# Holding back the second half of batch 1's stacks in the first attention's prologue

## The chip, the cores and the metric

The kernel runs on one core of one Trainium2 chip. The metric is the device time of one execution in microseconds (us). A core has TensorE (PE, matrix products and transposes into PSUM), VectorE (DVE), ScalarE (ACT), GpSimd (POOL) and SyncE (SP), each with an instruction stream of its own, joined by semaphores, and 16 DMA engines that all of them share. SP and POOL issue DMAs here.

## The reference

Two blocks of gated attention and feed-forward over x (8 batches of 256 tokens, width 256) and a context of the same shape. The change touches the first attention alone:

```
x = x + tanh(g_xattn[0]) * attention(layernorm(x), ctx, ctx)
  q = layernorm(x) @ Wq + bq;  k = ctx @ Wk + bk;  v = ctx @ Wv + bv       16 heads of 16
  softmax(q k^T / 4) v, heads side by side, @ Wo + bo
x = x + tanh(g_ffn[0]) * slots(layernorm(x))          (a routed slot layer with a GRU)
x = x + tanh(g_xattn[1]) * attention(layernorm(ctx), layernorm(ctx) and layernorm(x))
x = x + tanh(g_ffn[1]) * quantised gated feed-forward(layernorm(x))
```

All is float32. Products that need more precision than one pass gives are made from a high and a low part of each operand.

## The kernel before, in words

`attention0` runs over the 8 batches in order. For each batch the context and the normalised x are turned by PE and projected to k and q. ACT takes the high part out of PSUM (`k_high`, `q_high`, L393), DVE the low part (`k_low`, `q_low`, L553), which raises the semaphores `k_lo` and `q_lo`. Then DMAs from SBUF to SBUF build "stacks": for each pair of heads the 16 rows of q and k stand three times under each other (high with high, high with low, low with high), so that one matmul with 48 rows makes the precise product. `place` issues them: 64 KB each, two per row group, so six for k and six for q for one half of the head pairs (pairs 0 to 3 are half 0, pairs 4 to 7 half 1). A batch needs four such groups of six, 24 DMAs.

A batch has eight head pairs (r = 0 to 7). PE makes `scores` of a pair (L815), DVE takes the row maxima (`pair_max`, L568), POOL splits the maxima of two pairs into a high and a low part (`split_max`, L322 and L324), PE turns them (`turn_max`, L835), ACT copies them out (`shift_out`, L413) and POOL writes them by two small DMAs as two more rows of the query stack (`shift_in`, L330). The `shifted_scores` (L828) are then the transposed scores less the maximum, made from 50 rows; ACT takes their exponential (L407), and `group` (L846) multiplies by v. Scores run six pairs ahead of the transposed ones (`AHEAD = 6`), so at r = 2 of batch b the scores of pair 0 of batch b + 1 are made, at r = 6 those of its pair 4. `fold_bias` (L856, once, at r = 7 of batch 0) needs Wo and bo.

Every engine follows an order written out by hand. PE's prologue ends with `scores(0, 0, 0)` to `scores(0, 0, 5)` with two `turn_max` between them, and then the loop over batches begins with `shifted_scores(0, 0, 0)`. SP issues, in this order: ctx 0, x 0, weights, ctx 1, x 1, `first_stacks()` (half 0 of batch 0's k, the high rows of its q, half 1 of its q), ctx 2, x 2, `stacks(1, 1, False)` (both halves of batch 1), bo, Wo, w1, w2, ctx 3, x 3, `stacks(2, 0, True)`, and so on. POOL places the last row group of q for half 0 of batch 0 (two DMAs, `first_q`) and half 1 of its k (six, `first_k`). Between batches SP waits for `k_lo` and `q_lo` of the batch to be placed.

In the rows, the tiles of the two key stacks are `c_kv` (even batches) and `a_k_stack` (odd batches), the query stack is `a_q_stack`, the parts that they are copied from, and the shifts, lie in `w_hi` and `w_lo`, and PSUM is `ab_ps`.

Of the kernel before, what the change touches and what calls it, by code (L numbers as in the profile page):

```python
# [42 lines left out]
HP = 2  # L43
# [28 lines left out]
def wait(eng, sem, count):  # L72

    if isinstance(count, int) and count <= 0:
        return
    eng.wait_ge(sem, count)


def pause(eng, sem, count, passed):

    eng.wait_ge(sem, count)
    if not isinstance(count, int):
        eng.sem_inc(passed, 1)


def flat(ap):
    return ap.rearrange("p a d -> p (a d)")
# [13 lines left out]
def attention0(nc, a, x_sb, ident, gates, gru, slot, xn1, shared, xT_first, ps):  # L101
# [7 lines left out]
    with ctx:  # L109
# [21 lines left out]
        k_parts, q_parts = (part(0, 2048 * i, 2048).rearrange("p (a b n) -> p a b n", a=2, b=2) for i in range(2))  # L131
        k_stack = (shared[2][:, :, :, :].rearrange("p a c n -> p (a c n)").rearrange("p (r t) -> p r t", r=NR), sb("a_k_stack", [P, NR, T], F32R)[:, :, :])
        q_stack = sb("a_q_stack", [P, 2, NR, T], F32R)
# [26 lines left out]
        s = {k: sem("a_" + k) for k in names}  # L160
# [16 lines left out]
        def in_order(batch):  # L177

            for b in range(B):
                batch(b, b % 2, done=b > 0, prep=b < B - 2, more=b < B - 1, old=b > 1)  # L180

        K_ROWS = ((0, 0), (2, 0), (1, 1))
        Q_ROWS = ((0, 0), (1, 0), (2, 1))

        def rows_of(stack, par, rows):
            return stack[par][rows, :, :] if isinstance(stack, tuple) else stack[rows, par, :, :]

        def place(eng, parts, stack, which, half, par, done):

            for i, part in which:  # L190
                for e in range(HP):
                    eng.dma_start(rows_of(stack, par, slice(64 * e + DK * i, 64 * e + DK * i + DK))[:, 4 * half:4 * half + 4, :].bitcast(F32),
                                  parts[64 * e:64 * e + 64, par, part, half * T:(half + 1) * T].bitcast(F32)).then_inc(done, DMA)
# [9 lines left out]
        def _(sp):  # L203
# [8 lines left out]
            def stacks(n, par, again):  # L212
                for half in range(2):
                    if later(n):
                        pause(sp, s[("stack0", "stack1")[half]], HALF * n - (2 * DMA, HALF // 2)[half], s["sp_passed"])
                    if again:
                        pause(sp, s["ST"], HP * (NR * n - 3 * NR // 2 + half * NR // 2), s["sp_passed"])
                    if half == 0:
                        pause(sp, s["k_lo"], n + 1, s["sp_passed"])
                    place(sp, k_parts, k_stack, K_ROWS, half, par, s[("stack0", "stack1")[half]])  # L220
                    if half == 0:
                        pause(sp, s["q_lo"], n + 1, s["sp_passed"])
                    place(sp, q_parts, q_stack, Q_ROWS, half, par, s[("stack0", "stack1")[half]])
# [5 lines left out]
            def first_stacks():  # L229

                sp.wait_ge(s["k_hi"], 1)
                place(sp, k_parts, k_stack, K_ROWS[:2], 0, 0, s["stack0"])
                sp.wait_ge(s["k_lo"], 1)
                place(sp, k_parts, k_stack, K_ROWS[2:], 0, 0, s["stack0"])
                sp.wait_ge(s["q_hi"], 1)
                place(sp, q_parts, q_stack, Q_ROWS[:2], 0, 0, s["stack0"])
                sp.wait_ge(s["q_lo"], 1)
                place(sp, q_parts, q_stack, Q_ROWS, 1, 0, s["stack1"])

            load_ctx(0)  # L240
# [53 lines left out]
        @block.gpsimd  # L294
        def _(pool):
            nc.gpsimd.memset(ident[:, :], 0.0).then_inc(s["ident0"], 1)
            pool.wait_ge(s["ident0"], 1)
            nc.gpsimd.affine_select(out=ident[:, :], in_=ident[:, :], compare_op=ALU.not_equal, fill=1.0, base=0,
                                    pattern=[[-1, P]], channel_multiplier=1).then_inc(s["ident"], 1)
            pool.memset(minus_half4[:, :], -0.5).then_inc(s["const"], 1)  # L300
            pool.memset(unit[:, :], 1.0).then_inc(s["unit"], 1)
            pool.wait_ge(s["unit"], 1)
            for e in range(HP):
                for par in range(2):
                    pool.dma_start(k_stack[par][64 * e + 3 * DK:64 * e + 3 * DK + 2, :, :].bitcast(F32),
                                   unit[:, None, :].broadcast_to([2, NR, T])).then_inc(s["units"], DMA)
            pool.memset(max_parts[:, :, :, :].bitcast(F32), 0.0).then_inc(s["zeros"], 1)
            pool.memset(v_ones[:, :, :, :, DK:VW], 1.0).then_inc(s["ones"], 1)
            pool.wait_ge(s["const"], 1)

            def rstd_of(n):
                pool.wait_ge(s["var"], n + 1)
                wait(pool, s["xn"], n)
                nc.gpsimd.tensor_tensor(rstd[:, :], var_eps[:, :], minus_half[:, :], ALU.pow).then_inc(s["rstd"], 1)

            def split_max(G, buf):

                columns = max_parts[:, buf, :, :].rearrange("p t (e c) -> p t e c", e=HP)
                pause(pool, s["max"], 4 * G + 4, s["pool_passed"])
                if not isinstance(G, int) or G >= 2:  # L320
                    pause(pool, s["turned"], G - 1, s["pool_passed"])
                nc.gpsimd.tensor_copy(columns[:, :, :, 0:2], neg_max[:, buf, :, :, :]).then_inc(s["parts"], 1)  # L322
                pool.wait_ge(s["parts"], 2 * G + 1)
                nc.gpsimd.tensor_tensor(columns[:, :, :, 2:4], neg_max[:, buf, :, :, :], columns[:, :, :, 0:2].bitcast(F32), ALU.subtract).then_inc(s["parts"], 1)  # L324

            def shift_in(G, g, par):

                pause(pool, s["shift"], G + 1, s["pool_passed"])
                for e in range(HP):
                    pool.dma_start(q_stack[64 * e + 3 * DK:64 * e + 3 * DK + 2, par, 2 * g:2 * g + 2, :].bitcast(F32),  # L330
                                   shift[64 * e:64 * e + 4, g % 2, :].bitcast(F32)).then_inc(s[("shifted0", "shifted1")[g % 2]], DMA)

            rstd_of(0)
            rstd_of(1)
            pool.wait_ge(s["zeros"], 1)
            pool.wait_ge(s["q_lo"], 1)
            place(pool, q_parts, q_stack, Q_ROWS[2:], 0, 0, s["first_q"])
            pool.wait_ge(s["k_lo"], 1)
            place(pool, k_parts, k_stack, K_ROWS, 1, 0, s["first_k"])
            split_max(0, 0)  # L340
            shift_in(0, 0, 0)
            split_max(1, 1)
            shift_in(1, 1, 0)
            split_max(2, 0)

            def batch(b, par, done, prep, more, old):
                if prep:
                    rstd_of(b + 2)
                shift_in(4 * b + 2, 2, par)
                for g in range(3, 7 if more else 4):  # L350
                    split_max(4 * b + g, g % 2)
                    if g < 6:
                        shift_in(4 * b + g, g % 4, par if g < 4 else 1 - par)

            in_order(batch)
            for p in range(NPAIR - 1):
                t4 = slice(4 * p, 4 * p + 4)
                pool.wait_ge(s["slot_var"], p + 1)
                nc.gpsimd.tensor_tensor(slot["rstd"][:, t4], slot["var_eps"][:, t4], minus_half4[:, :], ALU.pow).then_inc(s["slot_rstd"], 1)
            pool.wait_ge(s["slot_rstd"], NPAIR - 1)  # L360
# [145 lines left out]
        def _(dve):  # L506
# [38 lines left out]
            def xnT_lo(n, bank):  # L545
                dve.wait_ge(s["xT_hi"], n + 1)
                nc.vector.tensor_tensor(xT_lo[:, :], bank[:, :], xT_hi[:, :].bitcast(F32), ALU.subtract).then_inc(s["xT_lo"], 1)
# [9 lines left out]
            def k_low(n, par, bank=pK):  # L557
                low(n, "k_hi", k_parts[:, par, :, :], bank, bkq[:, 0, :], "k_lo")

            def q_low(n, par, bank=pK):  # L560
                low(n, "q_hi", q_parts[:, par, :, :], bank, bkq[:, 1, :], "q_lo")

            def pair_max(n, G, r):

                wait(dve, s["parts"], 2 * G - 2)
                for e in range(HP):
                    dve.wait_ge(s["S"], 2 * n + e + 1)
                    nc.vector.tensor_reduce(neg_max[:, r // 2 % 2, :, e, r % 2], pS[:, e, :, :], AX_X, ALU.max, negate=True).then_inc(s["max"], 1)  # L568
# [161 lines left out]
            nc.vector.tensor_copy(bv_wide[:, :, :], bv_col[:, :, None].broadcast_to([P, DC, P])).then_inc(s["bvw"], 1)  # L730
            xnT_lo(1, flat(pT[:, 1, :, :]))
            k_low(1, 1, pP)
            q_low(1, 1, pK)
            pair_max(0, 0, 0)
            pair_max(1, 0, 1)
            pair_max(2, 1, 2)
            pair_max(3, 1, 3)
# [2137 lines left out]
```

## Time and profile before

| | us |
|---|---|
| median of 3 runs (lowest, highest) | 858.06 (855.92, 859.29) |
| the profiled execution, its own time | 858.11 |
| its span, first to last instruction | 856.0 |
| PE busy | 800.6 (94%) |
| DVE busy | 660.9 |
| ACT busy | 593.2 |
| POOL busy | 126.6 |

The span is what the profiler sees; the 2.1 us between it and the time lie around it. The first attention takes about the first 195 us. Its prologue, up to the first transposed scores, is the only part of it in which PE isn't busy nearly all the time.

### The profile page before, as it was taken

What the parts mean: (1) busy time and instruction counts of PE and PEld (TensorE: products, weight loads), DVE (VectorE), ACT (ScalarE), POOL (GpSimd) and SP (SyncE); (2) the same over time, 40 slices, a digit from 0 to 9 for tenths busy, and PEclk for the clock granted to TensorE, in tenths of its full rate; (3) what the DMA queues carried; (4) which work ended last, traced back from release to release, by engine and by line L of the source; (5) the groups of instructions that cost most, each with busy time, mean ns of one, the idle gap of its engine ahead of it and who ended that gap; (6) DMA issues with size and microseconds to landing.
All of it is one profiled execution on the core that took longest, in us unless ns stands there. A gap on an engine that the chain in (4) does not pass through costs nothing. (4 is left out here: it accounts for less than half of the span.)

```text
span 856.0 us, 15678 instructions
## 1 busy us (share of the span) xinstructions
PE 800.6 (94%) x5425; PEld 647.8 (76%) x5427; DVE 660.9 (77%) x1518; ACT 593.2 (69%) x1231; POOL 126.6 (15%) x229
## 2 busy tenths in 40 slices
PE   5799999999897999999999999999999999999667
PEld 5577777666465887888888888888888888888223
DVE  5678888886795878877876877877886886777587
ACT  5277777675634777777777777777777777777665
POOL 4333333330010001000000000000000000000645
PEclk9699999999899999999999999999999999999878
DMA  4734344215005000000000000000000000000002
GB/s 133 133 120 132 120 131 132 84 47 162 1 0 169 13 1 1 13 1 1 14 1 1 13 2 1 13 1 1 15 1 1 1 1 1 1 1 1 1 1 99
DMA packets 40605, 33.49 MB, mean 39 GB/s; under 512 B 12672, under 2 KB 38848, under 8 KB 40528
## 3 DMA queue, kind: packets, MB, share of 16 engines
q1 hardware_dynamic: 38032, 31.63, 12.7%
q0 software_dynamic: 2496, 0.87, 0.7%
q8 instruction: 44, 0.72, 0.4%
q14 instruction: 33, 0.27, 0.1%
HBM read 17.46 MB, written 2.10 MB: 23 GB/s over the span
## 5 line engine op out<-in xcount | busy, mean ns | idle before, releaser
L1994 DVE TENSOR_REDUCE c_neg_max<-c_pS 128x1 f32<-128x512 f32 x127 | 87.6, 690 | 59.8 <-PE c_pS L2335 57.7
L1787 ACT ACTIVATE c_probs<-c_pS,c_neg_max 128x512 f32<-128x512 f32 x127 | 87.5, 689 | 57.0 <-DVE c_neg_max L1994 57.0
L568 DVE TENSOR_REDUCE a_neg_max<-ab_ps 128x2 f32<-128x512 f32 x128 | 82.5, 687 | 29.2 <-PE ab_ps L815 28.6
L1805 ACT ACTIVATE c_probs<-c_probs,c_r_sum 128x512 f32<-128x512 f32 x126 | 91.0, 722 | 3.4 <-DVE c_r_sum L2000 2.2
L407 ACT ACTIVATE a_probsT<-ab_ps 128x512 f32<-128x512 f32 x128 | 70.3, 608 | 26.0 <-PE ab_ps L828 25.6
L1978 DVE TENSOR_TENSOR c_pT_lo<-c_pT,c_pT_hi 128x512 fp32r<-128x512 f32 x125 | 85.2, 681 | 0.0
L2292 PE MATMUL c_pK<-c_kv,w_hi 128*128 128x512 f32 x256 | 80.4, 395 | 4.4 <-PEq L1615 3.8
L2320 PE MATMUL c_pK<-w_hi,c_kv 128*128 128x512 f32 x248 | 79.4, 401 | 1.8 <-DVE c_k_lo L1962 1.7
L2362 PE MATMUL c_pO<-c_pT_hi,c_v_hi 128*128 128x256 f32 x248 | 75.3, 304 | 2.0 <-DVE c_pT_lo L1978 2.0
L2349 PE MATMUL c_pT<-ident,c_probs 128*128 128x128 f32 x508 | 76.0, 272 | 0.0
L2349 PEld LDWEIGHTS c_pT<-ident,c_probs 128*128 128x128 f32 x508 | 62.9, 140 | 17.1 <-ACT c_probs L1805 0.4
L1795 ACT CAST c_pT_hi<-c_pT 128x512 fp32r<-128x512 f32 x125 | 72.1, 577 | 0.0
L2362 PE MATMUL c_pO<-c_pT_hi,c_v_lo 128*128 128x256 f32 x248 | 70.0, 282 | 0.0
L2362 PE MATMUL c_pO<-c_pT_lo,c_v_hi 128*128 128x256 f32 x248 | 69.6, 281 | 0.0
L2292 PEld LDWEIGHTS c_pK<-c_kv,w_hi 128*128 128x128 f32 x256 | 48.2, 189 | 16.1 <-issue 4.2
L1973 DVE TENSOR_TENSOR c_v_lo<-c_pK,c_v_hi 128x512 fp32r<-128x512 f32 x62 | 42.9, 692 | 21.4 <-ACT c_v_hi L1779 21.4
L2320 PEld LDWEIGHTS c_pK<-w_hi,c_kv 128*128 128x128 f32 x248 | 45.1, 188 | 17.1 <-DVE c_k_lo L1962 7.7
L1962 DVE SCALAR_TENSOR_TENSOR c_k_lo<-c_pK,c_bk,c_k_hi 128x512 fp32r<-128x512 f32 x64 | 47.3, 739 | 10.0 <-ACT c_k_hi L1768 10.0
L1800 ACT ACTIVATE c_oT_hi<-c_pO,c_bv 128x256 fp32r<-128x256 f32 x63 | 29.9, 475 | 35.0 <-PE c_pO L2362 35.0
L2307 PE MATMUL c_pQ<-c_kv,w_hi 128*128 128x256 f32 x256 | 54.0, 303 | 0.0
L2335 PE MATMUL c_pS<-c_k_hi,c_q_hi 128*128 128x512 f32 x127 | 51.9, 408 | 0.0
L2292 PE MATMUL c_pK<-c_kv,w_lo 128*128 128x512 f32 x128 | 50.5, 395 | 0.0
(422 smaller groups left out, 2060.1 us busy)
## 6 DMA issues: line engine op xcount, KB each, us to landing
a_q_stack<-w_hi SPq DMA_DIRECT2D x94, 64.0 KB, 2.6
a_k_stack<-w_hi SPq DMA_DIRECT2D x48, 64.0 KB, 2.7
c_kv<-w_hi SPq DMA_DIRECT2D x42, 64.0 KB, 2.6
s_ctx<-in_ctx_dram SPq DMA_DIRECT2D x8, 256.0 KB, 4.0
x_sb<-in_x_dram SPq DMA_DIRECT2D x8, 256.0 KB, 4.3
ctx_in<-in_ctx_dram SPq DMA_DIRECT2D x8, 256.0 KB, 2.7
out_dram<-x_sb SPq DMA_DIRECT2D x7, 256.0 KB, 2.2
a_q_stack<-w_lo POOLq DMA_DIRECT2D x64, 4.0 KB, 2.4
```

Source lines behind the costliest of these rows:

```text
L407: nc.scalar.activation(probsT[:, r // 2 % 2, 2 * (r % 2) + e, :, :], pT[:, e, :, :], ACT.Exp).then_inc(s["exp"], 1)
L568: nc.vector.tensor_reduce(neg_max[:, r // 2 % 2, :, e, r % 2], pS[:, e, :, :], AX_X, ALU.max, negate=True).then_inc(s["max"], 1)
L1787: nc.scalar.activation(probs[:, u % 2, :], bank, ACT.Exp, bias=neg_max[:, u % 4:u % 4 + 1], accum_out=sums[:, u % 4:u % 4 + 1]).then_inc(s ...
L1795: nc.scalar.copy(dst[:, :, half], (pT[:, u % 2, :] if bank is None else bank).rearrange("p (t q) -> p t q", q=P)).then_inc(s["T_hi"], 1)
L1805: nc.scalar.mul(probs[:, u % 2, :], probs[:, u % 2, :], r_sum[:, u % 4:u % 4 + 1]).then_inc(s["probs"], 1)
L1978: nc.vector.tensor_tensor(dst[:, :, half], (pT[:, u % 2, :] if bank is None else bank).rearrange("p (t q) -> p t q", q=P), high[:, :, half ...
L1994: nc.vector.tensor_reduce(neg_max[:, u % 4:u % 4 + 1], pS[:, u % 2, :] if bank is None else bank, AX_X, ALU.max, negate=True).then_inc(s[" ...
L2292: last = nc.tensor.matmul(pK[:, :], W[x][:, c, INNER + h * DH:INNER + (h + 1) * DH], kv[par][:, y, c, :], start=(c == 0 and i == 0), stop= ...
L2307: last = nc.tensor.matmul(pQ[:, 0:T], W[x][:, c, h * DH:(h + 1) * DH], kv[par][:, y, c, T:KEYS], start=(c == 0 and i == 0), stop=(c == DC ...
L2320: last = nc.tensor.matmul(bank[:, :], kv[par][:, y, c, kt * P:(kt + 1) * P], W[x][:, c, 2 * INNER + half * 512:2 * INNER + (half + 1) * 51 ...
L2349: last = nc.tensor.transpose(bank[:, t * P:(t + 1) * P], probs[:, u % 2, t * P:(t + 1) * P], ident[:, :])
L2362: last = nc.tensor.matmul(bank[:, 0:T], (v_hi, v_lo)[x][:, h // 4, t, (h % 4) * DH:(h % 4 + 1) * DH], (high, low)[y][:, t, :], start=(t == ...
```

## The change

The second half of batch 1's stacks, and with it all that SP issues behind it, waits until the first head of the third transposed scores of batch 0 is done (`ST` counts heads, two per pair, so 2 * HP + 1 = 5). The last row group of batch 0's first query half is issued by SP instead of POOL, behind the high rows and ahead of half 1. DVE takes the first pair's maximum ahead of `q_low(1)` instead of behind it. Everything that is computed stays the same.

```diff
@@ def stacks(n, par, again), SP
                     if again:
                         pause(sp, s["ST"], HP * (NR * n - 3 * NR // 2 + half * NR // 2), s["sp_passed"])
+                    if n == 1 and half == 1:
+                        sp.wait_ge(s["ST"], 2 * HP + 1)
                     if half == 0:
                         pause(sp, s["k_lo"], n + 1, s["sp_passed"])
@@ def first_stacks(), SP
                 place(sp, q_parts, q_stack, Q_ROWS[:2], 0, 0, s["stack0"])
                 sp.wait_ge(s["q_lo"], 1)
+                place(sp, q_parts, q_stack, Q_ROWS[2:], 0, 0, s["first_q"])
                 place(sp, q_parts, q_stack, Q_ROWS, 1, 0, s["stack1"])
@@ POOL
             pool.wait_ge(s["zeros"], 1)
-            pool.wait_ge(s["q_lo"], 1)
-            place(pool, q_parts, q_stack, Q_ROWS[2:], 0, 0, s["first_q"])
             pool.wait_ge(s["k_lo"], 1)
             place(pool, k_parts, k_stack, K_ROWS, 1, 0, s["first_k"])
@@ DVE
             k_low(1, 1, pP)
+            pair_max(0, 0, 0)
             q_low(1, 1, pK)
-            pair_max(0, 0, 0)
             pair_max(1, 0, 1)
```

## Rows read from the trace of the kernel before

**Rows 1.** The page, part 1: busy time, share of the span, instructions

```profile
PE 800.6 (94%) x5425; PEld 647.8 (76%) x5427; DVE 660.9 (77%) x1518; ACT 593.2 (69%) x1231; POOL 126.6 (15%) x229
```

**Rows 2.** Stretches: length, busy us per engine, granted clock, DMA share, GB/s

```profile
24.50:31.80 7.30, 6.39 (x22) 4.30 (x21) 5.36 (x9) 0.75 (x2) 2.38 (x7) 0.50 1.14 183
...
29.00:32.50 3.50, 2.72 (x10) 1.83 (x9) 2.50 (x5) 0.37 (x1) 1.49 (x4) 0.50 1.12 150
...
31.80:34.70 2.90, 0.00 (x0) 0.02 (x1) 2.02 (x7) 0.00 (x0) 1.73 (x5) 0.50 0.62 121
34.70:41.00 6.30, 6.29 (x34) 5.40 (x34) 3.82 (x7) 3.02 (x6) 1.51 (x4) 0.54 0.34 102
...
74.80:94.90 20.10, 19.82 (x201) 14.74 (x200) 16.44 (x34) 14.45 (x33) 6.44 (x16) 1.00 0.40 127
```

**Rows 3.** Timeline of PE: start, duration, instruction, [idle before, ended by]

```profile
22.24 0.51 PE L815 MATMUL ab_ps<-c_kv,a_q_stack 48*128 48x256 f32 x4 [1.16 <-DMA a_q_stack<-w_hi]
...
34.71 0.80 PE L828 MATMUL ab_ps<-a_q_stack,c_kv 50*128 50x256 f32 x4 [3.00 <-DMA a_q_stack<-w_lo]
...
41.01 0.51 PE L828 MATMUL ab_ps<-a_q_stack,c_kv 50*128 50x256 f32 x4
...
50.78 0.40 PE L815 MATMUL ab_ps<-a_k_stack,a_q_stack 48*128 48x256 f32 x4
...
53.15 1.13 PE L856 MATMUL ab_ps<-a_wo,a_bv_wide 128*128 128x256 f32 x4
...
60.18 0.40 PE L815 MATMUL ab_ps<-c_kv,a_q_stack 48*128 48x256 f32 x4
```

**Rows 4.** Timeline of POOL, its DMA issues in the prologue

```profile
18.32 1.08 POOL L192 DMA_DIRECT2D a_q_stack<-w_hi  x2 [5.54 <-DVE w_hi L553]
19.39 3.02 POOL L192 DMA_DIRECT2D c_kv<-w_hi  x6
...
27.82 1.13 POOL L330 DMA_DIRECT2D a_q_stack<-w_lo  x2 [1.62 <-ACT w_lo L413]
```

**Rows 5.** DMA issues of short stretches: issuer, count, KB each, median us to landing

```profile
c_kv<-w_hi POOLq DMA_DIRECT2D x6, 64.0 KB, 4.6
...
a_q_stack<-w_lo POOLq DMA_DIRECT2D x1, 4.0 KB, 4.9
...
a_q_stack<-w_lo POOLq DMA_DIRECT2D x2, 4.0 KB, 5.5
...
a_q_stack<-w_lo POOLq DMA_DIRECT2D x2, 4.0 KB, 2.2
...
c_kv<-w_hi SPq DMA_DIRECT2D x6, 64.0 KB, 2.7
...
a_wo<-in_L_xattn_Wo_dram SPq DMA_DIRECT2D x1, 256.0 KB, 4.8
...
x_sb<-in_x_dram SPq DMA_DIRECT2D x1, 256.0 KB, 4.8
```

**Rows 6.** Timeline of SP's issues (idle time isn't shown for it)

```profile
16.84 6.32 SPq L192 DMA_DIRECT2D a_q_stack<-w_hi  x10
...
32.65 3.78 SPq L192 DMA_DIRECT2D a_k_stack<-w_hi  x6
...
41.17 0.43 SPq L258 DMA_DIRECT2D a_wo<-in_L_xattn_Wo_dram  x1
...
43.37 0.47 SPq L227 DMA_DIRECT2D x_sb<-in_x_dram  x1
48.78 4.13 SPq L192 DMA_DIRECT2D c_kv<-w_hi  x6
53.38 3.74 SPq L192 DMA_DIRECT2D a_q_stack<-w_hi  x6
```

**Rows 7.** Timeline of DVE

```profile
12.70 0.88 DVE L553 SCALAR_TENSOR_TENSOR w_hi<-ab_ps,a_bkq,w_hi 128x256 fp32r<-128x256 f32 x2 [0.70 <-ACT w_hi L393]
...
21.99 0.88 DVE L553 SCALAR_TENSOR_TENSOR w_hi<-ab_ps,a_bkq,w_hi 128x256 fp32r<-128x256 f32 x2 [0.97 <-ACT w_hi L393]
...
24.36 1.29 DVE L568 TENSOR_REDUCE a_neg_max<-ab_ps 128x2 f32<-128x512 f32 x2 [0.29 <-PE ab_ps L815]
...
54.86 0.74 DVE L521 BATCH_NORM_STATS2 a_stats<-x_sb 128x6 f32<-128x256 f32 x2
```

## The prediction

> **What bounds the kernel now.** I read the page first: TensorE (PE) is busy for 94% of the span [rows 1], so a change to the start of the first attention can matter only where PE stands still or runs slowly. The view by stretches shows where that is. In the steady loop a batch takes 20.1 us with 19.82 us of matmuls in it: PE bound. The weak place is the prologue: no matmul at all runs from 31.8 to 34.7, the granted clock is 0.50 (1.2 GHz) in the stretches around it, and the DMA engines' share is 1.14 from 24.5 to 31.8, which is saturation [rows 2]. The timeline of PE names the end of that idle time: 3.00 us until a DMA into the query stack from w_lo, which is `shift_in(0, 0, 0)`, GpSimd's (POOL's) two 4 KB transfers of the row maxima [rows 3]. POOL had started them at 27.82 and about 28.4 [rows 4]. The first landed after 4.9 us and the mean of the two is 5.5, so the second took 6.1 us and landed at 34.5; the same pair of transfers takes 2.2 us at 38 us, when the queues are short [rows 5]. So 3 us of PE are lost to a backlog in the DMA engines. What feeds it are SyncE's (SP's) back-to-back issues and POOL's six 64 KB key placements, issued from 19.39 to 22.41, which took 4.6 us each to land [rows 4, 5, 6].
>
> Then I asked who has slack. SP needs 3.7 to 4.1 us for six placements [rows 6]; four such groups and three loads make some 17 us per batch of 20.1. SP is the next bound behind PE, and the change makes it stand still.
>
> **The change part by part.**
>
> *The last query part of batch 0 goes from POOL to SP.* Two issues are added to SP and two taken from POOL. SP's ten issues took 6.32 us, 0.63 each [rows 6]. The moved ones come fifth and sixth: the second starts at 16.84 + 5 x 0.63 = 20.0 and, with a landing between 2.7 (the unloaded row) and 3.5 us, is there at 22.7 to 23.5; I take 22.8. Before, PE started the scores at 22.24 [rows 3]: 0.5 us later. All that SP issues behind it (second half of batch 0's query, ctx 2, x 2, first half of batch 1) moves back by 1.3 us. The Trainium skill, "DMA: Bandwidth & Descriptors", "Issuing engines are not separate DMA queues", says that spreading issues over engines saves only sequencer time, usually small beside the DMA. By that rule this edit would be free and the start 0.5 us earlier than I have it. I count the issues in full, because in the rows SP's issue time is what nearly fills a batch: 24 placements at 0.63 are 15.1 us of 20.1.
>
> *POOL's key part moves forward.* `k_lo(0)` is there at 13.58 [rows 7], so the six placements start at about 14.2 instead of 19.39 (POOL needed 0.6 us after its wait at 17.73, too [rows 4]). They have until the fifth scores at 28.7 and land by 22 at the latest; nothing waits for them. What they free is the saturated stretch: 384 KB, which at its mean of 183 GB/s [rows 2] is 2.1 us of all engines, and 2.6 us at the 150 GB/s that was moved from 29 to 32.5, when hardly anything but placements was under way and the share was still 1.12 [rows 2].
>
> *`pair_max(0, 0, 0)` ahead of `q_low(1)`.* Before, `q_low(1)` ran at 21.99 in time in which VectorE (DVE) had nothing else to do, and the second maximum began at 24.36 [rows 7]. Now the first maximum starts at 23.1 (22.8 and half of the first matmuls), ends at 24.4, `q_low` takes 0.88, and the second maximum starts at 25.3: 0.9 us later. Had the scores not been late, it would be 0.4. What `q_low(1)` releases (SP's first half of batch 1) is issued only after 29, so its own delay costs nothing. The ping-pong of scores and maxima up to 31.8 has no slack longer than some tenths, so the sixth scores end about 0.8 us late, at 32.5; bounds 0.3 and 0.9.
>
> *The landing of the first shift.* It is issued 0.8 us later, the second transfer at 29.2. With POOL's 2.6 us of backlog gone, 6.1 becomes 3.5 us and it lands at 32.7, hardly after PE is free. The bounds are 2.2 (no backlog) and 6.1 (no help). So the first transposed scores start at 32.75 instead of 34.71. From there PE had 6.30 us of uninterrupted work to the third transposed scores at 41.01 [rows 2, 3]; DVE, also 0.8 us late, adds 0.3 at the seventh scores. The third starts at 39.35: **1.65 us gained so far**.
>
> *The new wait.* SP stops before the second half of batch 1 until the first head of the third transposed scores is through, at 39.65. Queued behind it: 12 placements, bo, Wo, w1, w2, ctx 3, x 3, then batch 2's stacks. Before, this sequence ran from 32.65 to 43.84, 11.19 us without a gap, and then SP was idle until 48.78, when `k_lo(3)` released it [rows 6]. That idle time is the cover, 4.9 us, and the wait takes 7.0. What comes late, each with its consumer less the gain so far:
> - second half of batch 1: the last placement starts 7.2 us in, lands 2.7 later [rows 5]: 49.55. Its scores stood at 50.78 [rows 3], now due at 49.13: PE waits 0.4, gain left 1.2.
> - Wo: issued 8.5 us in, landing 4.8 [rows 5, 6]: 52.97. `fold_bias` stood at 53.15 [rows 3], due at 51.95: PE waits 1.0, gain left 0.2.
> - x 3: issued 10.7 us in, 4.8 to land: 55.2. DVE's statistics stood at 54.86 [rows 7], due at 54.7. DVE is 0.5 late, the next scores still find their maximum.
> - batch 2, first half: keys start at 39.65 + 11.19 = 50.9 and take 4.13 with 0.05 of gap around them; queries follow at 55.05, the last starts 3.1 in and lands 2.7 later: 60.9. Its scores stood at 60.18 [rows 3, 6]. **PE is 0.7 us late.**
>
> These aren't added: PE works in order, and the last one decides. Behind it the slack returns: SP is 1.7 us late at the end of the queries (58.8 against 57.1), PE 0.7; the second half of batch 2 lands about 69.5 for scores due at 71.2, and at batch 3 SP waits for `k_lo` again. The 0.7 us stay to the end, because the loop is PE bound [rows 2].
>
> **Sum.** The profiled execution took 858.11 us for a span of 856.0; the median of the runs is 858.06, the same within their spread (855.92 to 859.29). 858.1 + 0.7 = **858.8 us**. Under 0.5%, 4.3 us, a measurement can hardly tell this kernel from no change, and all that the prologue's idle time offers (3.0 us) is less than that.
>
> **The rivals.**
> *A, the gain stays.* SP's groups of six vary between 3.7 and 4.1 us, and the shift may land after 2.2 instead of 3.5 us, so that PE isn't held there. If the third transposed scores start at 38.3 and SP needs 0.7 us less than I have it, batch 2's queries land at 59.1, 1.1 us before 60.18: 857.0. If SP's chain doesn't decide at all, the 1.65 us stay (856.4), or 2.7 of them (855.4). I put this case at 856.4. Against it: there are four late deliveries in a row, and one is enough.
> *B, the landing isn't shortened.* Then the third transposed scores start at 41.01 + 0.8 = 41.8, SP at 42.1, batch 2's queries land at 63.4, 3.2 us after 60.18: 861.3. It decides if the shift takes over 5.5 us to land. For it: SP issues 64 KB each 0.63 us, 1.3 us later than before, straight through that time. The Trainium skill, "DMA: Bandwidth & Descriptors", "Queues, rings and completion order", says that each DMA engine goes round its queues packet by packet; by this rule POOL's small transfer never stood behind SP's backlog, and shortening the backlog need not shorten it. The trace speaks against the rule in this use: 6.1 us against 2.2 with and without backlog [rows 5].
> *C, the clock falls again (the slower side).* PE's clock was down for some 16 us, from 24.5 to about 40.5, after a stretch with gaps at the scores. The new waits are at 49, 52 and 60. At the low clock the same group of matmuls takes 0.80 instead of 0.51 us [rows 3]; 16 us of it do the work of 10.2: 5.8 us more, 864.6. It decides if the granted clock shows 0.5 anywhere behind 49 us. Against it: the waits are 0.4 to 1.0 us, in between PE is busy without a gap, while before the fall its share was far lower.
>
> **Chances.** Main case (858.8) 0.50, with 857.6 to 860.3 as its own range (below: the scores start 0.5 us earlier and SP needs 0.7 less; above: the shift lands after 5.0 us instead of 3.5); A 0.28; B 0.14; C 0.05; a gain over 4.3 us, which would need the clock's fall to be avoided altogether (the low clock costs about 2.3 us of the 6.3 from 34.7 to 41) on top of the 3 us, 0.03. Range 855.6 to 861.4. Faster by over 0.5%: 0.03. Slower by over 0.5%: C and the end of B, 0.06. The rest, 0.91, is within.
>
> **What will show it.** In the profile after: POOL's key issues at 14.2; first scores at 22.8 and the second maximum at 25.3; the first transposed scores at 32.75 with little or no wait for a DMA from w_lo; the third at 39.35; SP idle from 33.9 to 39.65; and PE waits for a DMA into the query stack at 49, for Wo's at 52, for the query stack at 60, the last one deciding; no clock under 1.00 behind 41 us. The prediction is wrong if the shift still lands after 34 or if SP's idle time of 4.9 us is longer than it looks, so that no PE wait appears behind 41 us.

## The result and the profile after

| | before | after |
|---|---|---|
| median of 7 runs (lowest, highest), us | 858.22 (852.74, 860.11) | 862.99 (860.98, 864.78) |
| ratio, 95% interval | | 1.0064 (1.0041 to 1.0086) |
| the profiled execution: time, span | 858.11, 856.0 | 864.78, 863.0 |
| the next stage's first load, in the profile | 200.03 | 208.14 |

The change made the kernel slower, by 4.8 us in the medians. The forecast was 858.8 us in a range that ended at 861.4. The profiled execution of after is the slowest of its seven; all its excess lies in the first attention, at whose end it is 8.1 us late (0.7 of that are there from the start, where the first projection began later; this differs from one execution to the next).

PE's timeline of after, to be held against [rows 3]. Idle time before an instruction and what ended it stand in brackets.

```profile
25.45 0.80 PE L816 MATMUL ab_ps<-c_kv,a_q_stack 48*128 48x256 f32 x4 [3.68 <-DMA a_q_stack<-w_hi]
...
35.02 0.45 PE L829 MATMUL ab_ps<-a_q_stack,c_kv 50*128 50x256 f32 x1
...
35.27 0.74 PE L829 MATMUL ab_ps<-a_q_stack,c_kv 50*128 50x256 f32 x3
...
42.47 0.51 PE L829 MATMUL ab_ps<-a_q_stack,c_kv 50*128 50x256 f32 x4
...
53.35 0.50 PE L816 MATMUL ab_ps<-a_k_stack,a_q_stack 48*128 48x256 f32 x4 [0.93 <-DMA a_q_stack<-w_hi]
...
55.83 1.13 PE L857 MATMUL ab_ps<-a_wo,a_bv_wide 128*128 128x256 f32 x4
...
61.95 1.39 PE L816 MATMUL ab_ps<-a_k_stack,a_q_stack 48*128 48x256 f32 x4 [1.59 <-DVE a_neg_max L569]
63.27 2.93 PE L799 MATMUL ab_ps<-w_lo,w_hi 128*128 128x256 f32 x12
...
67.57 0.63 PE L816 MATMUL ab_ps<-c_kv,a_q_stack 48*128 48x256 f32 x4
```

The wait of 3.00 us for the shift is gone: the first transposed scores follow on the scores at 35.0. But the wait at the first scores has grown from 1.16 to 3.68 us, and they are 3.2 us late. The third transposed scores are 1.5 us late instead of 1.65 early. From there the lateness grows: 2.6 us at 53.35 (50.78 before), 4.7 at 61.95 (57.24 before), 7.4 at 67.57 (60.18 before), and then it stays near 8. SP's and DVE's timelines and the DMA issues of after say what the steps are:

```profile
17.52 7.55 SPq L192 DMA_DIRECT2D a_q_stack<-w_hi  x12
...
43.05 3.74 SPq L192 DMA_DIRECT2D a_k_stack<-w_hi  x6
...
51.28 1.21 SPq L261 DMA_DIRECT2D a_wo<-in_L_xattn_Wo_dram  x1
...
54.25 0.47 SPq L229 DMA_DIRECT2D x_sb<-in_x_dram  x1
54.83 3.75 SPq L192 DMA_DIRECT2D c_kv<-w_hi  x6
58.62 4.10 SPq L192 DMA_DIRECT2D a_q_stack<-w_hi  x6
```

```profile
60.05 0.75 DVE L522 BATCH_NORM_STATS2 a_stats<-x_sb 128x6 f32<-128x256 f32 x2 [2.44 <-DMA x_sb<-in_x_dram]
...
61.20 1.29 DVE L569 TENSOR_REDUCE a_neg_max<-ab_ps 128x2 f32<-128x512 f32 x2
```

```profile
a_wo<-in_L_xattn_Wo_dram SPq DMA_DIRECT2D x1, 256.0 KB, 4.3
...
x_sb<-in_x_dram SPq DMA_DIRECT2D x1, 256.0 KB, 5.8
```

SP resumes at 43.05 and issues x 3 at 54.25, 11.2 us later; before, 10.7 us lay between [rows 6]. The half microsecond more comes mainly from the issue of Wo, 1.21 us long instead of 0.43. x 3 takes 5.8 us to land, not 4.8 [rows 5]: DVE stands still for 2.44 us with a row maximum queued behind its statistics, and PE waits 1.59 us for that maximum. Wo lands in 4.3 us, and PE doesn't wait for it. Then the view by stretches (busy us of PE, PEld, DVE, ACT, POOL; granted clock; DMA share; GB/s) shows the rest:

```profile
21.80:25.40 3.60, 0.00 (x0) 0.00 (x0) 0.00 (x0) 0.93 (x3) 0.00 (x0) 0.92 1.18 139
...
31.00:35.00 4.00, 3.36 (x13) 2.51 (x15) 2.67 (x5) 0.74 (x2) 1.51 (x4) 0.50 0.32 103
...
42.50:53.00 10.50, 9.64 (x101) 7.09 (x100) 6.51 (x11) 8.29 (x20) 3.01 (x8) 1.00 0.31 85
53.00:60.00 7.00, 6.44 (x66) 4.09 (x68) 3.66 (x7) 3.56 (x8) 1.51 (x4) 1.00 0.89 215
60.00:69.60 9.60, 7.91 (x48) 5.85 (x48) 6.10 (x15) 3.75 (x9) 2.25 (x5) 0.64 0.33 98
...
61.95:69.60 7.65, 7.55 (x44) 5.69 (x44) 4.27 (x9) 1.81 (x5) 1.67 (x5) 0.55 0.28 86
```

PE's granted clock is 1.00 (2.4 GHz) again from 42.5, but 0.64 on average from 60 to 69.6, after the stall: the 12 matmuls of L799 take 2.93 us instead of 1.70 in the same place before. The lateness grows there from 4.7 to 8.1 us: 3.4 us are the clock's.

### The profile page after: what moved, and what is told of

Read it like the earlier page. It is cut to its first block and busy times, and to the rows that moved or that the text cites. A ratio compares the mean times of both kernels' runs of the same rounds, so it can differ in the third digit from the quotient of the medians.

```text
span 863.0 us, 15681 instructions
## 1 busy us (share of the span) xinstructions
PE 804.7 (93%) x5427; PEld 650.6 (75%) x5427; DVE 659.9 (76%) x1518; ACT 592.7 (69%) x1231; POOL 125.7 (15%) x227
## 5 line engine op out<-in xcount | busy, mean ns | idle before, releaser
L2363 PE MATMUL c_pO<-c_pT_lo,c_v_hi 128*128 128x256 f32 x248 | 69.6, 281 | 0.0
```

The source lines that it names most:

```text
L2363: last = nc.tensor.matmul(bank[:, 0:T], (v_hi, v_lo)[x][:, h // 4, t, (h % 4) * DH:(h % 4 + 1) * DH], (high, low)[y][:, t, :], start=(t == ...
```

## The experiments

All are the kernel before with some of the change's parts, or with variants of them. Each was timed in five rounds against the kernel before on the same chip. "Next stage" is when the next stage's first load is issued in the one profiled execution (200.03 before); one execution can be late there when the median isn't (b2, c4), and from there to the end the executions differ by up to 3.5 us in no order that follows the edits. So the last column is the measure, and a profile shows what can happen and why. The kernel before had medians of 857.56 beside the runs a, 858.23 beside b and 858.20 beside c.

| run | what | next stage | median us | ratio (95%) |
|---|---|---|---|---|
| after | all three parts | 208.14 | 862.99 | 1.0064 (1.0041 to 1.0086) |
| a1 | SP's wait alone | 203.38 | 861.79 | 1.0061 (1.0038 to 1.0083) |
| a2 | query part on SP, POOL's keys early | 200.28 | 857.07 | 0.9999 (0.9981 to 1.0017) |
| a3 | query part on SP, POOL's keys held | 200.02 | 858.01 | 1.0013 (0.9997 to 1.0030) |
| a4 | all but the wait | 200.47 | 857.27 | 1.0001 (0.9981 to 1.0021) |
| b1 | POOL: keys first, then the query part | 200.43 | 857.81 | 0.9999 (0.9984 to 1.0014) |
| b2 | query part on SP, keys after the first scores | 202.94 | 857.34 | 0.9990 (0.9974 to 1.0005) |
| b3 | wait for the first transposed scores | 200.21 | 858.19 | 0.9988 (0.9974 to 1.0002) |
| b4 | SP's wait, other loads out of its way | 200.78 | 858.47 | 0.9997 (0.9984 to 1.0009) |
| c1 | wait and query part, no early maximum | 208.33 | 862.79 | 1.0061 (1.0037 to 1.0085) |
| c2 | all three, other loads out of the way | 202.39 | 858.07 | 1.0011 (0.9993 to 1.0030) |
| c3 | wait ahead of the first half instead | 198.47 | 856.24 | 0.9990 (0.9971 to 1.0009) |
| c4 | as c3, w1 and w2 later | 205.30 | 856.53 | 0.9989 (0.9969 to 1.0009) |

### a1: the wait alone

```diff
+                    if n == 1 and half == 1:
+                        sp.wait_ge(s["ST"], 2 * HP + 1)
```

> The kernel before with SP's new wait alone. Theory 1 (the wait is what costs): the third transposed scores stay at 41.0, SP resumes at 41.6, its chain of 11.2 us ends with x 3 issued at 52.8 and landed at about 58.4 (5.65 us, as in the changed kernel); DVE waits for it some 3.5 us, the scores behind it are 3 us late, PE's clock falls to 1.2 GHz near 60 and gives about 3 us more: 4 to 6.5 us slower. Rival (the late first scores, not the wait, cost the time): within 1 us of before, no clock fall behind 42 us.

Measured: 1.0061, the whole loss. PE's timeline of a1, and its DMA issues from 47.9 to 51.2:

```profile
33.48 0.80 PE L830 MATMUL ab_ps<-a_q_stack,c_kv 50*128 50x256 f32 x4 [1.98 <-DMA a_q_stack<-w_lo]
...
39.76 0.51 PE L830 MATMUL ab_ps<-a_q_stack,c_kv 50*128 50x256 f32 x4
...
55.00 1.10 PE L858 MATMUL ab_ps<-a_wo,a_bv_wide 128*128 128x256 f32 x4 [2.70 <-DMA a_wo<-in_L_xattn_Wo_dram]
```

```profile
a_wo<-in_L_xattn_Wo_dram SPq DMA_DIRECT2D x1, 256.0 KB, 6.3
...
x_sb<-in_x_dram SPq DMA_DIRECT2D x1, 256.0 KB, 7.4
```

Here the wait even does what it is for: the first transposed scores start 1.2 us earlier and the third transposed scores start at 39.76 instead of 41.01. (In b4, the same wait with bo and Wo issued ahead of it, PE still waits 2.55 us for the shift.) But Wo, issued at 48.56, takes 6.3 us to land and PE stands still for 2.70 us; x 3 takes 7.4. The stretch behind it runs at the lower clock:

```profile
52.30:55.00 2.70, 0.01 (x1) 0.03 (x1) 1.39 (x3) 1.06 (x3) 1.52 (x4) 1.00 0.87 288
55.00:59.50 4.50, 4.50 (x31) 2.62 (x32) 1.65 (x7) 1.08 (x2) 0.00 (x0) 0.65 0.48 128
```

Where theory 1 expected x 3 as the delivery that decides, it was Wo: DVE waited 1.64 us for x 3 as well, but its maximum was ready just before PE, already held up by Wo, came for it. In after Wo landed in 4.3 us instead of 6.3, and PE came later, having waited 0.93 us for batch 1's queries: Wo was in time and x 3 wasn't.

### a2, a3 and a4: the other parts

```diff
 a2, SP:    +                place(sp, q_parts, q_stack, Q_ROWS[2:], 0, 0, s["first_q"])
 a2, POOL:  -            pool.wait_ge(s["q_lo"], 1)
            -            place(pool, q_parts, q_stack, Q_ROWS[2:], 0, 0, s["first_q"])
 a3: as a2, but POOL keeps   pool.wait_ge(s["q_lo"], 1)   ahead of its keys
 a4: the changed kernel without the two lines of a1
```

> The kernel before with the query part on SP and so POOL's keys at 14 us, nothing else. Theory 1 (the keys ahead of SP's queries build a backlog in the DMA engines): first scores near 24.8, 2.5 us late, but no wait for the first shift; third transposed scores within 1 us of before; no stall behind; total -0.5 to +1 us. Rival (SP's order alone delays the first scores): the same late start here, and in the run with the keys held too.

> The query part on SP, but POOL still waits for q_lo of batch 0 before it places its keys, which then start near 18.3 instead of 14. Theory 1 (backlog of the early keys): first scores near 22.8 to 23.3 instead of 24.8; the first shift lands late again, as before (6 us), so the total is within 1 us of before. Rival (SP's order): first scores at 24.8 here too.

> The changed kernel without SP's new wait (query part on SP and first maximum first). Theory 1: first scores near 24.8, second maximum 0.9 us later still, no clock fall behind 42 us, 0.5 to 2 us slower than before and at least 3 us faster than the changed kernel. Rival (the wait is harmless): as slow as the changed kernel, 4.8 us over before.

All three are level with the kernel before. PE's timelines of a2, and below it of a3, show why the query part neither gains nor costs:

```profile
24.48 0.80 PE L814 MATMUL ab_ps<-c_kv,a_q_stack 48*128 48x256 f32 x4 [3.49 <-DMA a_q_stack<-w_hi]
...
33.95 0.70 PE L827 MATMUL ab_ps<-a_q_stack,c_kv 50*128 50x256 f32 x3
...
41.30 0.51 PE L827 MATMUL ab_ps<-a_q_stack,c_kv 50*128 50x256 f32 x4
```

```profile
24.64 0.80 PE L815 MATMUL ab_ps<-c_kv,a_q_stack 48*128 48x256 f32 x4 [3.90 <-DMA a_q_stack<-w_hi]
```

The 3 us of idle time before the first transposed scores have moved to the first scores. a3 didn't tell the two explanations apart: with the keys held to 17.98 the first scores were as late, which the order theory had asked for, but POOL's keys still ran beside SP's queries. The early maximum (a4 against a2, c1 against after) changed nothing that can be measured; the second maximum came 0.4 us later in a4 than in a2.

### b1 and b2: what delays the first scores

```diff
 b1, POOL:
-            pool.wait_ge(s["q_lo"], 1)
-            place(pool, q_parts, q_stack, Q_ROWS[2:], 0, 0, s["first_q"])
             pool.wait_ge(s["k_lo"], 1)
             place(pool, k_parts, k_stack, K_ROWS, 1, 0, s["first_k"])
+            pool.wait_ge(s["q_lo"], 1)
+            place(pool, q_parts, q_stack, Q_ROWS[2:], 0, 0, s["first_q"])
 b2: as a2, and on POOL
+            pool.wait_ge(s["S"], 1)
             pool.wait_ge(s["k_lo"], 1)
```

> The kernel before with POOL's two pieces swapped: keys at 14, then the query part at 18.3 as before; SP's order as before, no new wait. If the backlog of POOL's keys is what made the first scores late, they are at 24 to 24.6 here. If it was SP's order (the query part issued fifth and sixth there), they stay at 22.3, and as the keys are gone from the later stretch the first shift lands by 31.7: up to 3 us faster than before.

> Query part on SP, POOL's keys only after the first scores have been made. Backlog theory: SP's queries meet no keys and the first scores come at 22.8; the keys then delay the first shift or the fifth scores, total within 1 to 3 us slower than before. Order theory: first scores at 24.6 again.

PE's timelines of b1 and of b2:

```profile
24.24 0.80 PE L815 MATMUL ab_ps<-c_kv,a_q_stack 48*128 48x256 f32 x4 [3.38 <-DMA a_q_stack<-w_hi]
```

```profile
23.75 0.51 PE L815 MATMUL ab_ps<-c_kv,a_q_stack 48*128 48x256 f32 x4 [1.35 <-DMA a_q_stack<-w_hi]
...
33.30 0.80 PE L815 MATMUL ab_ps<-c_kv,a_q_stack 48*128 48x256 f32 x4 [3.37 <-DMA c_kv<-w_hi]
```

b1 leaves SP's order as it was, and the first scores are late all the same: the keys make them late. In b2 the keys are out of the way; SP began its queries at 17.87 in that execution, so the sixth started at 17.87 + 5 x 0.63 = 21.0, and the scores came 2.7 us later, at 23.75: the unloaded landing of [rows 5]. The order theory falls. b2 pays at the fifth scores instead, 3.37 us until the keys are there. At each of the places tried for the six keys (from 19.4, 14 and 24.8 us), with SP's order of work unchanged around them, PE stood still for about 3 us once.

### b3, b4 and c2: what in the wait costs

```diff
 b3:
+                    if n == 1 and half == 1:
+                        sp.wait_ge(s["ST"], 1)
 b4 (c2: the same, with the change's other parts):
+                    if n == 1 and half == 1:
+                        sp.dma_start(bo ...); sp.dma_start(wo ...)      # from behind the stacks
+                        sp.wait_ge(s["ST"], 2 * HP + 1)
...
                 stacks(2 * i + 2, 0, True)
+                if i == 0:
+                    sp.dma_start(w1 ...); sp.dma_start(w2 ...)          # from ahead of ctx 3
```

> The kernel before with SP's wait at the first head of the first transposed scores instead of the third. SP resumes near 34 instead of 32.65, 1 to 1.5 us late, well inside its idle time of 4.9 us before batch 2: theory 1 expects no stall behind 42 us, the first shift about 1 us earlier (as with the wait alone) and a total 0 to 1.5 us faster than before. Rival (any wait there costs): over 2 us slower.

> SP's new wait alone, but bo and Wo are issued ahead of it, and w1 and w2 behind batch 2's first half, so that only the 12 placements, ctx 3 and x 3 stand behind the wait. Theory 1 (what costs is Wo and x 3 landing late, and the clock that falls after these stalls): neither PE waits for Wo nor DVE for x 3, no clock fall behind 42 us, total within 1 us of before, 3 us or more faster than the wait alone. Rival (the late stacks cost it): at least 2.5 us slower than before, with PE waiting for the query stack near 50 or 60.

> The changed kernel with bo and Wo ahead of the wait and w1, w2 behind batch 2's first half. Theory 1: x 3 is issued 2.6 us earlier behind the wait, DVE waits for it under 0.5 us instead of 2.4, PE's clock stays at 2.4 GHz behind 42 us, and the total is 0 to 2 us over before instead of 4.8. Rival (the second half's own lateness, 0.93 us of PE's wait near 52, makes the clock fall): still over 3 us slower.

A wait that ends some 6 us earlier (b3: SP resumes at 34.79, against 40.34 in a1) costs nothing. The full wait costs nothing either once only the stacks, ctx 3 and x 3 are behind it (b4), and taking those four loads out of the way brings the changed kernel back from 1.0064 to 1.0011. c2's timelines of SP and DVE, and its clock:

```profile
50.06 0.47 SPq L231 DMA_DIRECT2D x_sb<-in_x_dram  x1
```

```profile
55.38 0.74 DVE L523 BATCH_NORM_STATS2 a_stats<-x_sb 128x6 f32<-128x256 f32 x2
```

```profile
53.00:60.00 7.00, 7.00 (x65) 5.46 (x65) 6.85 (x18) 4.84 (x11) 3.37 (x8) 1.00 0.33 99
60.00:69.60 9.60, 8.91 (x94) 6.30 (x93) 6.67 (x14) 6.83 (x17) 2.10 (x7) 1.00 0.30 91
```

DVE no longer waits for x 3, and the clock stays at 1.00. Batch 2's queries still make PE wait, for 0.42 us (0.22 in b4), the kind and size of delay that the prediction had as the deciding one. In b4 and c2 x 3 is issued 8.2 us behind the end of the wait, 2 to 3 us sooner than in a1 and after, and Wo ahead of the wait; no run shows either alone.

### c1: without the early maximum

The wait and the query part, with `q_low(1)` ahead of the first maximum as before.

> The changed kernel with q_low ahead of the first maximum as before (so the wait and the query part on SP, without the third part). Theory 1: first scores late as in the changed kernel, the second maximum 0.4 to 0.9 us earlier, the stalls behind the wait as there: 4 to 5 us slower than before. Rival (the order of the first maximum matters): over 1.5 us faster than the changed kernel, that is at most 3 us over before.

1.0061, as the changed kernel. PE's timeline of c1:

```profile
52.88 0.51 PE L816 MATMUL ab_ps<-a_k_stack,a_q_stack 48*128 48x256 f32 x4 [1.25 <-DMA a_q_stack<-w_hi]
...
56.63 1.10 PE L857 MATMUL ab_ps<-a_wo,a_bv_wide 128*128 128x256 f32 x4 [1.20 <-DMA a_wo<-in_L_xattn_Wo_dram]
...
62.10 1.39 PE L816 MATMUL ab_ps<-a_k_stack,a_q_stack 48*128 48x256 f32 x4 [1.45 <-DVE a_neg_max L569]
```

DVE waits 2.01 us for x 3. The granted clock is still 1.00 from 53 to 60, behind the first of these waits and around the second, and 0.64 from 60 to 69.6, around the third. So the fall of the clock shows in all three profiles in which the four loads stand behind the full wait (after, a1, c1), with the late start and without it.

### c3 and c4: the wait where the backlog is

```diff
 c3:
+                    if n == 1 and half == 0:
+                        sp.wait_ge(s["shift"], 1)
 c4: also w1 and w2 behind stacks(2, 0, True), as in b4
```

> The kernel before with SP's wait ahead of batch 1's first half, until the first shift has been copied out (27.5), and none at the second half. The backlog is then worked off when the shift's small transfers are issued: they land in 2.2 to 3 us, PE's wait of 3.0 us goes, the third transposed scores start near 38.3. SP resumes 3.2 us later than before, inside its 4.9 us of idle time before batch 2, so nothing is late behind it. Theory 1: 2 to 3 us faster than before. Rival (SP has no room, or the backlog isn't the cause of the slow landing): no gain, with PE waiting for the query stack near 38, or for the shift as before.

> As the run with the wait at the first half, with w1 and w2 moved behind batch 2's first half, which takes 1.1 us off SP's chain before ctx 3 and x 3. Theory 1: the same as that run if SP's room was enough, up to 1 us faster if batch 2's stacks were late there.

PE's timeline of c3, and its DMA issues from 28.3 to 29.5:

```profile
31.96 0.80 PE L830 MATMUL ab_ps<-a_q_stack,c_kv 50*128 50x256 f32 x4
...
38.79 0.51 PE L830 MATMUL ab_ps<-a_q_stack,c_kv 50*128 50x256 f32 x4
```

```profile
a_q_stack<-w_lo POOLq DMA_DIRECT2D x2, 4.0 KB, 2.9
```

The mechanism is there as expected: with SP's next 12 placements held back until the shift is copied out, its transfers land in 2.9 us instead of 4.9 and 6.1, PE doesn't wait for them, and the third transposed scores start 2.2 us earlier than before. The 2 to 3 us that were expected of the total aren't there, though: the ratio is 0.9990 and its interval holds 1. In c3's profile 0.7 of the 2.2 us are gone again by 58.7; x 3, issued 4.4 us later than before and with batch 2's keys right behind it, made DVE wait 0.59 us ahead of that. c4's profile shows how more can be lost: the second 4 KB transfer of a shift, issued at 47.62 among ctx 3, x 3 and batch 2's keys, took 7.8 us to land, held PE for 3.23 us until 55.5, and the clock fell. c3 has the lowest median of all, but its ratio is no better than those of b2, b3 and c4, and no version is shown to be faster than the kernel before.

## Why the prediction was wrong

**The deciding step: "the new wait".** Its list of late deliveries was the right list, and the cause of the whole loss is there (a1 against a4). The term that failed is x 3's. DVE was to be 0.5 us late, and "the next scores still find their maximum". DVE waited 2.44 us, and its slack was only some 0.85 us: 1.59 us of it reached PE, in front of scores that were reckoned free of any wait. Of the 1.9 us too little, 1.0 is the landing (4.8 us assumed, 5.8 measured), 0.5 the issue of Wo, which was long in this execution, 0.3 SP's slower release behind the third transposed scores (0.58 us after their start, not 0.3), and the rest DVE's being due a little sooner.

The landing was taken from before, where batch 2's placements came 4.9 us behind x 3. The profiles show what makes it longer. It was 4.1 to 4.9 us in the seven profiles in which those placements came over 2 us behind x 3 (before, a2, a3, a4, b1, b2, b3). It was 5.5 to 7.4 us in the five in which they came right behind it and bo and Wo shortly ahead (c3, after, c1, c4, a1). It was 3.5 and 5.0 us in the two in which they came right behind it but the weights were out of the way (c2, b4). By these single executions it takes both neighbours. Wo's landing was mis-sized in a1 alone (6.3 us; 4.3 in after and 4.8 in c1, about as assumed).

**What was called rival C happened.** The clock, put at no cost in the sum, fell once PE had stood still for 1.6 us (after) or 2.7 us (a1). It was given 0.05, because the waits were reckoned at 0.4 to 1.0 us. It cost 3.4 us in the profile of after, against the 5.8 reckoned: 7.65 us at a mean granted clock of 0.55, not 16 us at the low one. Stall and clock together make the loss; which share each has in the 4.8 us of the medians isn't shown, since the profiled execution lost more than the others.

**The first scores: 25.45 instead of 22.8.** The step that failed is the landing of SP's sixth query placement, 2.7 to 3.5 us in the prediction and 4.8 us in after (issued at about 20.7), and behind it the sentence on POOL's early keys that "nothing waits for them". Nothing waits for the keys themselves until 28.7, but they make a backlog in front of SP's queries (b1, b2); 0.7 us of the lateness were there before any of this. The wait of 3.00 us for the shift did go, as predicted, and so did its cause; but the gain of 1.65 us was paid for in full at the first scores. Alone this is worth nothing either way (a2, a4: 0.9999 and 1.0001), so it isn't what made the kernel slow. It took away the gain that the prediction had set against the wait.

**The early maximum:** 0.9 us were expected at the second maximum. Beside the other parts it was 0.4, the figure without the late scores, and it can't be seen in the total.

**The scores at 60.18, 0.7 us late:** the step itself was about right, as b4 and c2 show, where the larger stalls are gone: totals of 0.9997 and 1.0011, with 0.22 and 0.42 us of PE's wait for the queries. In after it was hidden behind the earlier stalls.

**Rival A** didn't occur; what it asks for (an early shift, and SP in time behind it) is c3. **Rival B** didn't either: the shift's landing fell to 2.5 us in after and 2.9 in c3, so it does depend on the backlog. The Trainium skill's rule of "DMA: Bandwidth & Descriptors", "Queues, rings and completion order", that a DMA engine goes round its queues packet by packet, doesn't keep a small transfer of POOL's clear of SP's backlog here: 6.1 us with it (7.8 in c4), 2.5 without.

**Left open:** why x 3's landing differs from 5.5 to 7.4 us under what looks like the same load; whether Wo or x 3 brings the larger part of the loss in executions without a profile; and whether c3 gains anything: 1.6 us at the next stage in its profile, but a ratio whose interval, 0.9971 to 1.0009, holds both that and nothing. How often the clock falls there in executions without a profile isn't known either: their clock is on record only as a mean over the span, 0.969 to 0.976 in after's seven and 0.970 to 0.980 in those of before beside a1, too close to tell.

## What to carry to other kernels

A wait put into a queue delays everything behind it: list those transfers with their consumers, and give each the landing time that it has among the transfers that it will meet, not among those that it met before. Hold back the transfers that form the backlog, and only those; weights that are merely next in the order should go ahead of the wait or far behind it. A stall on PE is to be priced with the clock's fall when it may be as long as those that brought it here (1.45 us in c1, 1.59, 2.70, and 3.23 in c4; single ones of 0.42, 0.93, 1.20 and 1.25 us didn't, but in the prologue before two of 1.16 and 0.78 us in a row stood ahead of the fall). And a transfer group that is moved earlier for room must be held against what is urgent at its new place.

## What the runs showed of the hardware

The placements (64 KB, read in rows of 1 KB, SBUF to SBUF) fill the DMA engines far below what loads from memory reach: in after, from 21.8 to 25.4, a share of 1.18 moved 139 GB/s, while from 31 to 35, without a backlog, 103 GB/s needed a share of 0.32. SP alone issues at about 104 GB/s (64 KB each 0.63 us). The difference of some 35 GB/s is all that was left for a backlog, so, as an estimate from these figures, the 384 KB of POOL's six transfers take some 11 us to be worked off while SP goes on; in after the engines were still full at 25.4, 7 us after POOL's last issue. With loads from memory among the work, the same engines moved 288 GB/s at a share of 0.87 (a1, 52.3 to 55).
